# Second pass of the attention scores on 64 rows in each half of TensorE

## The chip, the cores and the metric

The kernel runs on one core of one Trainium2 chip. The metric is the device time of that core in microseconds (us), as the median of several runs. TensorE (PE in the profile) multiplies, VectorE (DVE), ScalarE (ACT) and GpSimd (POOL) do the element work, and SyncE (SP) issues the DMAs.

## The reference

The input `x` has shape (4, 512, 1024). It is layer-normalised to `xn`. An attention block and a gate are computed from `xn`, and the result is `x + attention * silu(gate)`. What the change touches is the scores of the attention, cut here to its core:

```python
q = (xn @ Wq).reshape(b, s, 16, 64)      # likewise k and v; rotary embedding on q and k
logits = einsum('bhqd,bhkd->bhqk', q, k) # 16 heads of dimension 64, 4 batches, 512 tokens
logits = where(causal, logits, -1e9) / sqrt(64)
attn = softmax(logits);  out = einsum('bhqk,bhkd->bhqd', attn, v);  out @ Wo
```

## The kernel before

All products are taken in `float32r`, whose multiplier keeps fewer bits than float32. So an operand is split in a high part (a rounded copy) and a low part (the difference), and a product is the sum high x high + high x low + low x high. `split_matmuls` (L44 to L46) writes these three matmuls for the projections and for the output product.

First the feed-forward block (lines 219 to 286) computes the gate of all tokens and leaves `xn` split in SBUF. Its router product (L231) runs with 32 columns of TensorE for each matmul, four of them beside each other. Then comes the attention loop: 32 steps, one for each pair of heads and each batch (`STEPS`); step `s` projects q, k and v of one pair (`project`, 3 x 8 x 3 matmuls of 128x512), and in between it computes what the projections of step `s-1` made possible: the scores of both heads, the softmax, the transposes of the probabilities (L1110) and their products with v (L1123). Two steps share one set of weights; in the second step of such a couple (`b == 1`) ACT and POOL split the next weights into `w_hi` (L1259) and `w_lo` (L1805). The loop is followed by a tail that finishes the last scores and forms the output product; in step 31 and the tail POOL splits `Wo` (L1809) too.

The scores of one head are causal, so the 128 queries of tile `t` meet `(t+1)*128` keys. `SCORE_BANKS` puts tile 3 (512 wide) in PSUM bank 0, tiles 2 and 0 (384 and 128 wide) in bank 1 and tile 1 (256 wide) in bank 2. The contraction has length 64, but the kernel uses all 128 rows. The stationary `q_st` of head `h` holds the high q on the head's own 64 rows and the low q on the other 64. The moving `k_hh` holds the high k on both halves: one matmul (L1092) gives high x high + low x high. A second one (L1093), with the same `q_st`, has the moving `k_l0`: the low k on the head's own rows and zeros on the others; it adds high x low. The two follow each other for each tile, and each bank is given free (`scored`) when its tiles are done.

The order of each engine is written out by hand in its `step`. What matters around the change:

- PE: projection 0 (first half), `v_transposes` (L1077), two probability transposes, projection 0 (second half), `values`, **`scores(s-1, 0)`**, projection 1, **`scores(s-1, 1)`**, eight transposes, projection 2 and so on. `scores` waits for `qk_ready` (two signals a step) and for the `Exp` of the bank's earlier use.
- DVE: `v_low` (L1516), `pt_low_parts` (L1544, 256 wide), `rotate_read(s, 0)` (L1498, L1499; it waits for projection 0), `merge` (L1552), the maxima of the scores (L1527), `normalise` (L1533, L1537), `q_low` (L1504; first `qk_ready`), `rotate_read(s, 1)`, the second head's maxima, `k_low` (L1511; second `qk_ready`), `pt_low_parts`.
- ACT: `exps` (L1297), `q_high` (L1266), `next_weights` of q in the steps with `b == 1`, the copies of the transposed probabilities (L1306), `k_high` (L1272), the other two `next_weights` (L1259), `v_hi` (L1286).
- POOL: `rotate` (L1797, L1801) of q and k, and in the steps with `b == 1` `weights_low` three times (L1805); the last two of these run into the next step.

The SP queue issues the weights' loads and the stores of each step. In the tail `load_rows(0)` waits for the last `qk_ready` and stands in that queue behind `load_wo(7)` and ahead of `load_att(2)` and the next stores.

Of the kernel before, what the change touches and what calls it, by code (L numbers as in the profile page):

```python
# [6 lines left out]
F32R = mybir.dt.float32r  # L7
ALU = mybir.AluOpType
ACT = mybir.ActivationFunctionType
AX = mybir.AxisListType  # L10

P = 128
# [23 lines left out]
def raw(ap):  # L36

    return ap.bitcast(F32)
# [670 lines left out]
def attention_block(nc, block, io, keep, xn, xn_store, z_store, att_store, out):  # L709
# [5 lines left out]
    with ExitStack() as ctx:  # L715
# [14 lines left out]
        with ExitStack() as loop_only:  # L730
            def lsb(name, shape, dt):
                return loop_only.enter_context(nc.sbuf_tensor(name, shape, dt))

            rotated = [lsb(f"at_rotated{c}", [P, SEQ], F32) for c in range(2)]
            v_t = lsb("at_v_t", [P, SEQ], F32)

            qk = lsb("at_qk", [P, 2, 6, SEQ], F32R)
            q_st, k_hh, k_l0 = ([[qk[:, p, c + h, :] for h in range(2)] for p in range(2)] for c in (0, 2, 4))

            v_hl = [lsb(f"at_v_hl{p}", [P, QT, 4, HEAD_DIM], F32R) for p in range(2)]  # L740
            neg_max = [lsb(f"at_neg_max{h}", [P, QT], F32) for h in range(2)]
            row_sum = [lsb(f"at_row_sum{h}", [P, QT], F32) for h in range(2)]
            inv_sum = [lsb(f"at_inv_sum{h}", [P, QT], F32) for h in range(2)]
            prob = [lsb(f"at_prob{h}", [P, 1280], F32) for h in range(2)]
            pt_hi = [lsb(f"at_pt_hi{h}", [P, 1280], F32R) for h in range(2)]
            pt_lo = [lsb(f"at_pt_lo{h}", [P, 1280], F32R) for h in range(2)]
            low_half = lsb("at_low_half", [P, SEQ], F32)
            att_t = [lsb(f"at_att_t{p}", [P, SEQ], F32) for p in range(2)]
            causal = lsb("at_causal", [P, SEQ], F32)
# [25 lines left out]
        w_high, w_ready, rope_in = keep["w_high"], keep["w_ready"], keep["rope_in"]  # L775

        xn_in, xn_ok = sem("at_xn_in"), keep["xn_ok"]
        zeroed = sem("at_zeroed")
        projected = sem("at_projected")
        rot_read, rot_a, rot_done = sem("at_rot_read"), sem("at_rot_a"), sem("at_rot_done")  # L780
        high_done, qk_ready = sem("at_high_done"), sem("at_qk_ready")
# [272 lines left out]
        def _(pe):  # L1054
# [25 lines left out]
            def scores(a, h, parity):  # L1080
                n = 2 * a + h
                pe.wait_ge(qk_ready, 2 * a + 2)
                if not later(a, 2):
                    pe.wait_ge(zeroed, 4)
                for bank, tiles in enumerate(SCORE_BANKS):
                    if later(n, 1):
                        pe.wait_ge(expd, 3 * (n - 1) + bank + 1)
                    for t, col in tiles:
                        width = (t + 1) * P
                        out = score_ps[bank][:, col:col + width]  # L1090
                        q = q_st[parity][h][:, t * P:(t + 1) * P]
                        pe.matmul(out, q, k_hh[parity][h][:, 0:width], start=True, stop=False)  # L1092
                        last = pe.matmul(out, q, k_l0[parity][h][:, 0:width], start=False, stop=True)  # L1093
                    last.then_inc(scored, 1)

            def prob_transposes(n, h, uses):
# [156 lines left out]
        def _(act):  # L1253
# [7 lines left out]
            def q_high(s, b):  # L1261
                act.wait_ge(rot_done, 2 * s + 1)
                if later(s, 2):
                    act.wait_ge(scored, 6 * (s - 1))
                for h, rows in enumerate(pair_rows):
                    last = act.activation(q_st[b][h][rows, :], rotated[0][rows, :], ACT.Copy)  # L1266
                last.then_inc(high_done, 1)

            def k_high(s, b, h):
                act.wait_ge(rot_done, 2 * s + 2)  # L1270
# [222 lines left out]
        def _(dve):  # L1493
            def rotate_read(s, c):
                dve.wait_ge(projected, 3 * s + c + 1)
                if later(s, 1):
                    dve.wait_ge(rot_done, 2 * s + c - 1)
                dve.tensor_tensor(turned[c][:], proj_ps[c][:], rope[:, 2 * c, :], ALU.mult)  # L1498
                dve.stream_shuffle(swapped[c][:], proj_ps[c][:], swap_mask).then_inc(rot_read, 1)  # L1499
# [8 lines left out]
            def k_low(s, b):  # L1508
                dve.wait_ge(high_done, 2 * s + 2)
                for h, rows in enumerate(pair_rows):  # L1510
                    last = dve.tensor_tensor(k_l0[b][h][rows, :], rotated[1][rows, :], raw(k_hh[b][h][rows, :]), ALU.subtract)  # L1511
                last.then_inc(qk_ready, 1)

            def v_low(a, parity):
# [4 lines left out]
            def maxima(n, h, banks=(0, 1, 2)):  # L1519
                for bank in banks:  # L1520
                    tiles = SCORE_BANKS[bank]
                    dve.wait_ge(scored, 3 * n + bank + 1)
                    dve.sem_inc(seen, 1)
                    dve.wait_ge(causal_ok, 2)
                    for t, col in tiles:
                        row = score_ps[bank][:, col:col + (t + 1) * P]
                        last = dve.tensor_tensor_reduce(out=row, in0=row, in1=causal[:, (QT - 1 - t) * P:SEQ], scale=-1.0,  # L1527
                                                        scalar=FAR, op0=ALU.add, op1=ALU.min, accum_out=neg_max[h][:, t:t + 1])
                    last.then_inc(maxed, 1)
# [10 lines left out]
            def pt_low_parts(n, h, uses=(0, 1, 2)):  # L1540
                for u in uses:
                    dve.wait_ge(pt_high, 3 * n + u + 1)
                    cols = slice(512 * u, 512 * u + PT_WIDTH[u])
                    dve.tensor_tensor(pt_lo[h][:, cols], pt_ps[u % 2][:, 0:PT_WIDTH[u]], raw(pt_hi[h][:, cols]),  # L1544
                                      ALU.subtract).then_inc(pt_ready, 1)
# [8 lines left out]
            def step(i, s, b):  # L1554
                if later(s, 1):
                    v_low(s - 1, 1 - b)
                if later(s, 2):
                    pt_low_parts(2 * s - 3, 1, (2,))
                rotate_read(s, 0)
                if later(s, 2):  # L1560
                    merge(s - 2, 2 * s - 3, 1, b)
                if later(s, 1):
                    maxima(2 * s - 2, 0)
                    normalise(2 * s - 2, 0)
                q_low(s, b)
                rotate_read(s, 1)
                if later(s, 1):
                    maxima(2 * s - 1, 1, (0,))
                    pt_low_parts(2 * s - 2, 0, (0,))
                    maxima(2 * s - 1, 1, (1, 2))  # L1570
                    pt_low_parts(2 * s - 2, 0, (1, 2))
                    normalise(2 * s - 1, 1)
                k_low(s, b)
                if later(s, 1):
                    pt_low_parts(2 * s - 1, 1, (0, 1))
                    merge(s - 1, 2 * s - 2, 0, 1 - b)

            dve.wait_ge(keep["z_add"], BATCH * QT)
            for p in range(2):
                dve.memset(raw(k_l0[p][0][HEAD_DIM:P, :]), 0.0).then_inc(zeroed, 1)  # L1580
                dve.memset(raw(k_l0[p][1][0:HEAD_DIM, :]), 0.0).then_inc(zeroed, 1)
            def wo_lo(k):
                dve.wait_ge(wo_high, k + 1)
                dve.tensor_tensor(wo_part[k][PLO], wo_raw[:, k % 3, :], raw(wo_part[k][PHI]), ALU.subtract).then_inc(wo_low_dve, 1)
# [1 line left out]
            def last_step(s, b):  # L1586

                v_low(s - 1, 1 - b)
                pt_low_parts(2 * s - 3, 1, (2,))
                rotate_read(s, 0)  # L1590
                merge(s - 2, 2 * s - 3, 1, b)
                maxima(2 * s - 2, 0)
                normalise(2 * s - 2, 0)
                q_low(s, b)
                rotate_read(s, 1)
                maxima(2 * s - 1, 1, (0,))
                pt_low_parts(2 * s - 2, 0, (0,))
                maxima(2 * s - 1, 1, (1, 2))
                pt_low_parts(2 * s - 2, 0, (1,))
                wo_lo(3)  # L1600
                pt_low_parts(2 * s - 2, 0, (2,))
                normalise(2 * s - 1, 1)
                k_low(s, b)
                pt_low_parts(2 * s - 1, 1, (0, 1))
# [108 lines left out]
            merge(s - 2, 2 * s - 4, 0, 0)  # L1713
            v_low(s - 1, 1)
            pt_low_parts(2 * s - 3, 1, (2,))
            maxima(2 * s - 2, 0)
            normalise(2 * s - 2, 0)
            merge(s - 2, 2 * s - 3, 1, 0)
# [75 lines left out]
        def _(pool):  # L1794
            def rotate(s, c):
                pool.wait_ge(rot_read, 2 * s + c + 1)
                pool.tensor_tensor(swapped[c][:], swapped[c][:], rope[:, 2 * c + 1, :], ALU.mult).then_inc(rot_a, 1)  # L1797
                pool.wait_ge(rot_a, 2 * s + c + 1)
                if later(s, 1):
                    pool.wait_ge(qk_ready, 2 * s + c - 1)  # L1800
                pool.tensor_tensor(rotated[c][:], swapped[c][:], turned[c][:], ALU.add).then_inc(rot_done, 1)  # L1801

            def weights_low(idx, m):
# [51 lines left out]
def later(count, least):  # L1855

    return not isinstance(count, int) or count >= least
# [94 lines left out]
```

## Time and profile before

| what | us |
|---|---|
| median of 3 runs (1139.3 to 1139.48) | 1139.34 |
| the profiled execution, its own time | 1140.27 |
| its span in the trace | 1138.5 |
| PE busy in the span | 1107.5 |
| DVE busy | 798.3 |
| ACT busy | 639.6 |
| POOL busy | 385.2 |

The rows further below come from the trace of the profiled execution, with times in us from the start of its span. Each row of a timeline is one instruction, or several of one kind merged (`x2`); its first number is its start and its second the time from there to the end. The duration that is shown for a matmul is modelled and overlaps the next one: what a matmul costs is read from one start to the next. `PEld` are the weight loads of TensorE; `[1.40 <-PE at_proj L46]` is idle time of the engine before the row and what ended it.

### The profile page before, as it was taken

What the parts mean: (1) busy time and instruction counts of PE and PEld (TensorE: products, weight loads), DVE (VectorE), ACT (ScalarE), POOL (GpSimd) and SP (SyncE); (2) the same over time, 40 slices, a digit from 0 to 9 for tenths busy, and PEclk for the clock granted to TensorE, in tenths of its full rate; (3) what the DMA queues carried; (4) which work ended last, traced back from release to release, by engine and by line L of the source; (5) the groups of instructions that cost most, each with busy time, mean ns of one, the idle gap of its engine ahead of it and who ended that gap; (6) DMA issues with size and microseconds to landing.
All of it is one profiled execution on the core that took longest, in us unless ns stands there. A gap on an engine that the chain in (4) does not pass through costs nothing.

```text
span 1138.5 us, 17762 instructions
## 1 busy us (share of the span) xinstructions
PE 1107.5 (97%) x5620; PEld 925.2 (81%) x5620; DVE 798.3 (70%) x1860; ACT 639.6 (56%) x1344; POOL 385.2 (34%) x240
## 2 busy tenths in 40 slices
PE   4899999999999999999999999999999999999998
PEld 3667777888888888888888888888888887788887
DVE  6768641476767776767776677767677768899865
ACT  6545542366665666646566565666656667645341
POOL 0443646352342433334342352523424335200000
PEclk9899999999999999999999999999999999999999
DMA  9526133220202202021460202202022014586764
GB/s 368 209 93 241 55 94 111 75 65 11 64 9 74 64 10 64 9 64 49 172 221 9 64 18 64 64 9 64 9 74 64 10 64 168 188 282 219 235 212 148
DMA packets 88719, 116.40 MB, mean 102 GB/s; under 512 B 3440, under 2 KB 69104, under 8 KB 87664
## 3 DMA queue, kind: packets, MB, share of 16 engines
q1 hardware_dynamic: 88688, 116.01, 30.4%
q8 instruction: 16, 0.26, 0.1%
q14 instruction: 15, 0.12, 0.0%
HBM read 82.44 MB, written 33.55 MB: 102 GB/s over the span
## 4 chain that ended last, share of the span: by engine, by line
PE 87%; DVE 6%; ACT 3%; issue 1%; POOL 1%; DMA 1%; SPq 0%; DVEq 0%; POOLq 0%; ACTq 0%
PE at_proj L44 17%; PE at_proj L46 17%; PE at_proj L45 17%; PE at_out L1123 7%; PE at_pt L1110 6%; PE ff_z_ps L286 5%; PE at_score L1092 4%; PE at_score L1093 3%; POOL ff_xs_lo L669 1%; PE at_pt L44 1%; PE at_pt L46 1%; PE at_pt L45 1%; PE at_proj L1077 1%; PE at_score L44 1%; PE at_score L45 1%
## 5 line engine op out<-in xcount | busy, mean ns | idle before, releaser
L44 PE MATMUL at_proj<-xn_hi,w_hi 128*128 128x512 f32 x824 | 333.6, 405 | 1.6 <-POOL w_lo L1813 0.8
L46 PE MATMUL at_proj<-xn_hi,w_lo 128*128 128x512 f32 x824 | 322.8, 392 | 0.0
L45 PE MATMUL at_proj<-xn_lo,w_hi 128*128 128x512 f32 x824 | 321.3, 390 | 0.0
L46 PEld LDWEIGHTS at_proj<-xn_hi,w_lo 128*128 128x128 f32 x824 | 154.6, 188 | 34.5
L1797 POOL TENSOR_TENSOR at_turning<-at_turning,rope_table 128x512 f32<-128x512 f32 x64 | 82.8, 1294 | 289.4 <-DVE at_turning L1499 289.4
L44 PEld LDWEIGHTS at_proj<-xn_hi,w_hi 128*128 128x128 f32 x824 | 154.9, 188 | 29.1 <-issue 1.2
L45 PEld LDWEIGHTS at_proj<-xn_lo,w_hi 128*128 128x128 f32 x824 | 155.3, 188 | 27.5
L1297 ACT ACTIVATE at_prob<-at_score,at_neg_max 128x512 f32<-128x512 f32 (+3 forms) x256 | 133.5, 526 | 71.2 <-DVE at_neg_max L1527 70.8
L1805 POOL TENSOR_TENSOR w_lo<-w_stage,w_hi 128x1024 fp32r<-128x1024 f32 x45 | 114.4, 2558 | 162.9 <-ACT w_hi L1259 162.9
L1306 ACT ACTIVATE at_pt_hi<-at_pt 128x512 fp32r<-128x512 f32 (+1 forms) x192 | 94.0, 524 | 99.7 <-PE at_pt L1110 98.9
L1544 DVE TENSOR_TENSOR at_pt_lo<-at_pt,at_pt_hi 128x512 fp32r<-128x512 f32 (+1 forms) x192 | 112.1, 598 | 42.1 <-ACT at_pt_hi L1306 41.1
L1527 DVE CUSTOM_DVE_ANT_0 at_score<-at_score,at_causal 128x512 f32<-128x512 f32 (+3 forms) x256 | 120.8, 514 | 1.0
L1110 PE MATMUL at_pt<-ident,at_prob 128*128 128x128 f32 x640 | 91.7, 274 | 0.8 <-DVE at_pt_lo L1544 0.6
L1313 ACT ACTIVATE at_low_half<-at_out 64x512 f32<-64x512 f32 x64 | 37.9, 592 | 96.8 <-PE at_out L1123 96.0
L1801 POOL TENSOR_TENSOR at_rotated<-at_turning 128x512 f32<-128x512 f32 x64 | 82.8, 1293 | 7.3 <-POOL at_turning L1797 4.4
L1511 DVE TENSOR_TENSOR at_qk<-at_rotated,at_qk 64x512 fp32r<-64x512 f32 x64 | 45.1, 705 | 56.4 <-ACT at_qk L1272 56.0
L286 PE MATMUL ff_z_ps<-sign_t,ff_xs_hi 128*128 128x512 f32 x256 | 83.4, 407 | 0.8 <-POOL ff_xs_lo L669 0.8
L1537 DVE TENSOR_SCALAR at_prob<-at_prob,at_inv_sum 128x256 f32<-128x256 f32 (+3 forms) x256 | 82.0, 384 | 2.3
L1272 ACT ACTIVATE at_qk<-at_rotated 64x512 fp32r<-64x512 f32 x128 | 80.5, 629 | 1.8 <-POOL at_rotated L1801 0.2
L286 PE MATMUL ff_z_ps<-sign_t,ff_xs_lo 128*128 128x512 f32 x256 | 81.4, 399 | 0.0
L1092 PE MATMUL at_score<-at_qk 128*128 128x512 f32 (+3 forms) x256 | 80.5, 328 | 0.0
L1110 PEld LDWEIGHTS at_pt<-ident,at_prob 128*128 128x128 f32 x640 | 73.0, 141 | 6.6 <-DVE at_pt_lo L1544 1.6
(214 smaller groups left out, 1924.9 us busy)
## 6 DMA issues: line engine op xcount, KB each, us to landing
w_stage<-_attn_hidden_states_dram SPq DMA_DIRECT2D x17, 512.0 KB, 6.4
z_store<-z SPq DMA_DIRECT2D x16, 512.0 KB, 2.8
w_stage<-in_L_attn_Wq_dram SPq DMA_DIRECT2D x16, 512.0 KB, 3.8
w_stage<-in_L_attn_Wk_dram SPq DMA_DIRECT2D x16, 512.0 KB, 5.1
w_stage<-in_L_attn_Wv_dram SPq DMA_DIRECT2D x16, 512.0 KB, 6.2
att_store<-at_att_t SPq DMA_DIRECT2D x32, 256.0 KB, 2.0
at_turning<-z_store SPq DMA_DIRECT2D x16, 512.0 KB, 5.4
w_stage<-in_L_attn_Wo_dram SPq DMA_DIRECT2D x12, 512.0 KB, 4.3
```

The costliest lines, as they stand in the source:

```text
L44: pe.matmul(out, sh, mh, start=first, stop=False, skip_group_check=reopened)
L45: pe.matmul(out, sh, ml, start=False, stop=False, skip_group_check=reopened)
L46: return pe.matmul(out, sl, mh, start=False, stop=final, skip_group_check=reopened)
L286: last = pe.matmul(z_ps[n % 2][:, o, :], part[:, k, tok], keep["sign_t"][:, k, o * HALF:(o + 1) * HALF], start=(k == 0 and part is xs_hi), ...
L1092: pe.matmul(out, q, k_hh[parity][h][:, 0:width], start=True, stop=False)
L1110: last = pe.transpose(pt_ps[u % 2][:, dst:dst + P], prob[h][:, src:src + P], keep["ident"][:])
L1297: last = act.activation(prob[h][:, P_COL[t]:P_COL[t] + width], score_ps[bank][:, col:col + width], ACT.Exp, scale=-1.0, bias=neg_max[h][:, ...
L1306: act.activation(pt_hi[h][:, 512 * u:512 * u + PT_WIDTH[u]], pt_ps[u % 2][:, 0:PT_WIDTH[u]], ACT.Copy).then_inc(pt_high, 1)
L1527: last = dve.tensor_tensor_reduce(out=row, in0=row, in1=causal[:, (QT - 1 - t) * P:SEQ], scale=-1.0, scalar=FAR, op0=ALU.add, op1=ALU.min, ...
L1544: dve.tensor_tensor(pt_lo[h][:, cols], pt_ps[u % 2][:, 0:PT_WIDTH[u]], raw(pt_hi[h][:, cols]), ALU.subtract).then_inc(pt_ready, 1)
L1797: pool.tensor_tensor(swapped[c][:], swapped[c][:], rope[:, 2 * c + 1, :], ALU.mult).then_inc(rot_a, 1)
L1805: pool.tensor_tensor(w_lo[m][:], w_raw[m], raw(w_hi[m][:]), ALU.subtract).then_inc(w_ready[m], 1)
```

## The change

The high part of q and both parts of k stay as they are in `q_st` and `k_hh`. The zero-padded `k_l0` is gone, with the four memsets that wrote its zeros. In its place are `k_own` (the low k of both heads, each on its own rows), `k_other` (the low k of each head, the first 384 keys, on the rows of the other head) and `q_other` (the high q of tiles 0 and 2 of each head, on the rows of the other head). The first pass of `scores` now makes the four matmuls of L1092 for all tiles, with 128 rows. The second pass makes four matmuls with 64 rows: tiles 3 and 1 on the head's own rows, tiles 2 and 0 on the other rows. `scored` is given in the second pass.

ACT makes two more copies in each `q_high` (64x256 each, behind the two that are there). DVE makes two more subtractions for each step (64x384 each), in the new `k_spread`. The second `qk_ready` of a step is given there; it is called one step later, ahead of `rotate_read(s, 0)`, and in the tail ahead of the maxima. `rotate` on POOL waits for the full `qk_ready` of the step before in both of its calls.

```diff
-            q_st, k_hh, k_l0 = ([[qk[:, p, c + h, :] for h in range(2)] for p in range(2)] for c in (0, 2, 4))
+            q_st, k_hh = ([[qk[:, p, c + h, :] for h in range(2)] for p in range(2)] for c in (0, 2))
+            k_own, k_other = ([qk[:, p, c, :] for p in range(2)] for c in (4, 5))
+            q_other = lsb("at_q_other", [P, 2, 2 * P], F32R)
+            OTHER_COL = {0: 0, 2: P}
+            OTHER_KEYS = 3 * P
...
             def scores(a, h, parity):
                 pe.wait_ge(qk_ready, 2 * a + 2)
...
-                        out = score_ps[bank][:, col:col + width]
-                        q = q_st[parity][h][:, t * P:(t + 1) * P]
-                        pe.matmul(out, q, k_hh[parity][h][:, 0:width], start=True, stop=False)
-                        last = pe.matmul(out, q, k_l0[parity][h][:, 0:width], start=False, stop=True)
+                        pe.matmul(score_ps[bank][:, col:col + width], q_st[parity][h][:, t * P:(t + 1) * P],
+                                  k_hh[parity][h][:, 0:width], start=(col == 0), stop=False, skip_group_check=True)
+                for bank, tiles in enumerate(SCORE_BANKS):
+                    for t, col in tiles:
+                        width = (t + 1) * P
+                        if t in OTHER_COL:
+                            q = q_other[other, parity, OTHER_COL[t]:OTHER_COL[t] + P]
+                            k = k_other[parity][other, 0:width]
+                        else:
+                            q = q_st[parity][h][own, t * P:(t + 1) * P]
+                            k = k_own[parity][own, 0:width]
+                        last = pe.matmul(score_ps[bank][:, col:col + width], q, k, start=False, stop=True,
+                                         skip_group_check=True)
                     last.then_inc(scored, 1)
...
             def q_high(s, b):
...
+                for h, rows in enumerate(pair_rows):
+                    act.activation(q_other[pair_rows[1 - h], b, :].rearrange("p (t n) -> p t n", t=2),
+                                   rotated[0][rows, :].rearrange("p (t a n) -> p t a n", t=2, a=2)[:, :, 0, :], ACT.Copy)
...
             def k_low(s, b):
                 dve.wait_ge(high_done, 2 * s + 2)
                 for h, rows in enumerate(pair_rows):
-                    last = dve.tensor_tensor(k_l0[b][h][rows, :], rotated[1][rows, :], raw(k_hh[b][h][rows, :]), ALU.subtract)
+                    dve.tensor_tensor(k_own[b][rows, :], rotated[1][rows, :], raw(k_hh[b][h][rows, :]), ALU.subtract)
+
+            def k_spread(b):
+                for h, rows in enumerate(pair_rows):
+                    last = dve.tensor_tensor(k_other[b][pair_rows[1 - h], 0:OTHER_KEYS], rotated[1][rows, 0:OTHER_KEYS],
+                                             raw(k_hh[b][h][rows, 0:OTHER_KEYS]), ALU.subtract)
                 last.then_inc(qk_ready, 1)
...
                     pt_low_parts(2 * s - 3, 1, (2,))
+                if later(s, 1):
+                    k_spread(1 - b)
                 rotate_read(s, 0)
...
                 if later(s, 1):
-                    pool.wait_ge(qk_ready, 2 * s + c - 1)
+                    pool.wait_ge(qk_ready, 2 * s)
```

## Rows read from the trace of the kernel before

**Rows 1.** The page, part 1: busy time of TensorE, share, instructions

```profile
PE 1107.5 (97%) x5620; PEld 925.2 (81%) x5620; DVE 798.3 (70%) x1860; ACT 639.6 (56%) x1344; POOL 385.2 (34%) x240
```

**Rows 2.** Windows, five steps: stretch, length, busy PE PEld DVE ACT POOL, clock, DMA

```profile
400.00:520.00 120.00, 120.00 (x637) 103.07 (x636) 85.18 (x223) 72.16 (x166) 42.26 (x26) 1.00 0.13 37
```

**Rows 3.** Timeline of PE, the scores of one second head (h = 1)

```profile
613.78 0.39 PE L1092 MATMUL at_score<-at_qk 128*128 128x512 f32 x1
...
614.23 0.33 PE L1092 MATMUL at_score<-at_qk 128*128 128x384 f32 x1
...
614.58 0.22 PE L1092 MATMUL at_score<-at_qk 128*128 128x128 f32 x1
614.64 0.27 PE L1093 MATMUL at_score<-at_qk 128*128 128x128 f32 x1
614.75 0.33 PE L1092 MATMUL at_score<-at_qk 128*128 128x256 f32 x1
614.92 0.28 PE L1093 MATMUL at_score<-at_qk 128*128 128x256 f32 x1
615.04 1.03 PE L1110 MATMUL at_pt<-ident,at_prob 128*128 128x128 f32 x8
```

**Rows 4.** Timelines of PE and PEld, narrow windows: into and out of the 32-column mode

```profile
147.59 0.40 PE L286 MATMUL ff_z_ps<-sign_t,ff_xs_lo 128*128 128x512 f32 x1
147.91 0.64 PE L231 MATMUL ff_small<-xn_full,ff_gate_raw 128*32 128x512 f32 x4
...
149.22 0.61 PE L231 MATMUL ff_small<-xn_full,ff_gate_raw 128*32 128x512 f32 x4
149.77 0.50 PE L286 MATMUL ff_z_ps<-sign_t,ff_xs_hi 128*128 128x512 f32 x1
150.10 0.40 PE L286 MATMUL ff_z_ps<-sign_t,ff_xs_hi 128*128 128x512 f32 x1
...
149.76 0.19 PEld L286 LDWEIGHTS ff_z_ps<-sign_t,ff_xs_hi 128*128 128x128 f32 x1 [0.84 <-issue]
```

**Rows 5.** Timeline of DVE: two steps of the loop, step 31, tail

```profile
606.05 0.69 DVE L1498 TENSOR_TENSOR at_turning<-at_proj,rope_table 128x512 f32<-128x512 f32 x1 [1.40 <-PE at_proj L46]
...
623.80 1.39 DVE L1511 TENSOR_TENSOR at_qk<-at_rotated,at_qk 64x512 fp32r<-64x512 f32 x2 [1.65 <-ACT at_qk L1272]
...
628.66 0.42 DVE L1544 TENSOR_TENSOR at_pt_lo<-at_pt,at_pt_hi 128x256 fp32r<-128x256 f32 x1
...
942.94 0.41 DVE L1544 TENSOR_TENSOR at_pt_lo<-at_pt,at_pt_hi 128x256 fp32r<-128x256 f32 x1
...
952.25 3.47 DVE L1504 TENSOR_TENSOR at_qk<-at_rotated,at_qk 64x512 fp32r<-64x512 f32 x2
...
969.05 0.42 DVE L1544 TENSOR_TENSOR at_pt_lo<-at_pt,at_pt_hi 128x256 fp32r<-128x256 f32 x1
```

**Rows 6.** Timeline of POOL: the splits of the weights (w_lo) and of Wo

```profile
626.66 4.75 POOL L1805 TENSOR_TENSOR w_lo<-w_stage,w_hi 128x1024 fp32r<-128x1024 f32 x2 [7.22 <-ACT w_hi L1259]
...
943.74 2.42 POOL L1809 TENSOR_TENSOR xn_lo<-w_stage,xn_hi 128x1024 fp32r<-128x1024 f32 x1 [10.51 <-ACT xn_hi L1318]
...
952.29 2.88 POOL L1809 TENSOR_TENSOR xn_lo<-w_stage,xn_hi 128x1024 fp32r<-128x1024 f32 x1 [1.15 <-DVE at_prob L1537]
...
967.42 2.40 POOL L1809 TENSOR_TENSOR xn_lo<-w_stage,xn_hi 128x1024 fp32r<-128x1024 f32 x1 [2.13 <-ACT xn_hi L1318]
```

**Rows 7.** Timeline of PE: first scores of a first head, three steps

```profile
631.18 0.45 PE L1092 MATMUL at_score<-at_qk 128*128 128x512 f32 x1
...
945.69 0.45 PE L1092 MATMUL at_score<-at_qk 128*128 128x512 f32 x1
...
968.35 0.48 PE L1092 MATMUL at_score<-at_qk 128*128 128x512 f32 x1
```

**Rows 8.** ACT: q_high's copies by line, and its next idle time

```profile
L1266 ACT ACTIVATE at_qk<-at_rotated x64: 623/628/632, 207.2 to 950.9; 64x512 fp32r<-64x512 f32 x64
...
615.68 1.09 ACT L1306 ACTIVATE at_pt_hi<-at_pt 128x512 fp32r<-128x512 f32 x2 [1.80 <-PE at_pt L1110]
```

More of the change, by code:

```diff
@@ L777, in attention_block @@
         xn_in, xn_ok = sem("at_xn_in"), keep["xn_ok"]
-        zeroed = sem("at_zeroed")
         projected = sem("at_projected")
@@ L1082, in scores @@
                 pe.wait_ge(qk_ready, 2 * a + 2)
-                if not later(a, 2):
-                    pe.wait_ge(zeroed, 4)
+                own, other = pair_rows[h], pair_rows[1 - h]
                 for bank, tiles in enumerate(SCORE_BANKS):
@@ L1578, in _ @@
             dve.wait_ge(keep["z_add"], BATCH * QT)
-            for p in range(2):
-                dve.memset(raw(k_l0[p][0][HEAD_DIM:P, :]), 0.0).then_inc(zeroed, 1)
-                dve.memset(raw(k_l0[p][1][0:HEAD_DIM, :]), 0.0).then_inc(zeroed, 1)
             def wo_lo(k):
@@ L1589, in last_step @@
                 pt_low_parts(2 * s - 3, 1, (2,))
+                k_spread(1 - b)
                 rotate_read(s, 0)
@@ L1715, in _ @@
             pt_low_parts(2 * s - 3, 1, (2,))
+            k_spread(1)
             maxima(2 * s - 2, 0)
```

## The prediction

> **What bounds the kernel now.** I read the page's shares first, then the windows of the loop, then the timeline of one step on each engine, and last the timelines where the loop ends. TensorE is busy for 97% of the span, DVE for 70%, ACT for 56% [rows 1]; in five steps of the loop TensorE has no idle time at all, at the full clock (granted 1.00, which is 2.4 GHz), while DVE is busy for 85.18 of 120 us, ACT for 72.16 and POOL for 42.26 [rows 2]. So in the loop the order of TensorE sets the time: whatever a step takes more or less there counts in full, and work of the other engines costs nothing as long as no wait of TensorE ends later for it. The change does something on both sides, so I price TensorE's instructions first and then look for the new waits.
>
> **The second pass on 64 rows.** A head's scores run from 613.78 to 615.04, 1.26 us [rows 3]. From starts: two 512-wide matmuls 0.45 (0.23 and 0.22), two 384-wide 0.35, the first 128-wide 0.06, the second 0.11, 256-wide 0.17 and 0.12. The weight loads explain the odd ones: a matmul that follows a 128-wide one comes only after about 0.11, since its load takes longer than 128 columns. After the change the first pass is 512, 384, 128, 256 in a row: 0.23 + 0.17 + 0.11 + 0.12 = 0.63. The second pass, if the halves work beside each other, is the longer of 0.23 (512, own rows) and 0.17 + 0.06 (384 and 128, other rows), then 256 on the own rows at 0.12: 0.35. Together 0.98, which is 0.28 less than now. Times 64 heads that is 17.9 us, the most that the halves can give.
>
> The trace has no 64-row matmul. The nearest thing is the router product, which runs in a mode of 128 rows and 32 columns [rows 4]. It shows that parts do work beside each other: four 512-wide matmuls start together at 147.91. It also shows what entering and leaving costs. Going in: the last full matmul starts at 147.59 and streams for 0.23, to 147.82; the first of the mode starts at 147.91, 0.09 later. Going out: the last four start at 149.22; between groups of four there are 0.43 us, so they end at 149.65; the next full-size weight load starts at 149.76 and not in the shade of the matmuls before it, 0.11 of nothing; the second full matmul follows the first by 0.33 instead of 0.23, so the load itself is exposed, 0.10 to 0.11. Each direction then costs 0.09 to 0.11 of emptiness and a full load of 0.11 that nothing hides. For one head: in 0.09 + 0.11, out 0.11 + 0.11, together 0.42. The head's scores become 0.63 + 0.20 + 0.35 + 0.22 = 1.40, against 1.26: **0.14 more for each head, 64 x 0.14 = 9.0 us**. Bounds: nothing for the mode gives -17.9; halves that do not overlap make the second pass 0.64 instead of 0.35, 0.43 a head more than now, +27.5. I take +9.0, as the only change of mode in the trace is priced like that.
>
> On this the Trainium skill, TensorEngine Tiling (Array Packing), Key Properties, says that changing the tiling mode drains TensorE while changing the tile does not. By that rule the switch costs in rows as in columns, and the trace agrees for columns, with the 0.09 and 0.11 us above; no row here shows it for rows.
>
> **k_spread on DVE.** Two subtractions of 64x384, both operands in SBUF. A pair of 64x512 takes 1.39, at 623.80 [rows 5], so one is about 0.69; 128x256 takes 0.42; 384 wide lies between, 0.56, and the pair is 1.13. Its place is behind `pt_low_parts` and ahead of `rotate_read(s, 0)`. In an odd step DVE idles there for 1.40, ahead of 606.05 [rows 5], so the pair fits: nothing. In an even step the idle time would nearly do as well, but POOL is at work: it splits the last two weights from 626.66 to 631.41 [rows 6], and k_spread is ready at 629.0, which is 628.66 + 0.42 less the overlap of two instructions [rows 5].
>
> What happens to a DVE instruction with two SBUF operands while POOL runs such a split is shown where the loop ends. The pair of q_low that starts at 952.25 takes 3.47 instead of 1.39; POOL's split started at 952.29 and ended at 955.17, and the pair ends at 955.72, 0.55 behind it [rows 5, 6]. The first of the pair got through, POOL took 2.88 instead of 2.40, and the second waited for POOL's end. So the later of the two waits for the earlier one. In even steps of the loop no DVE instruction with both operands in SBUF meets POOL's last two splits today; k_spread will. Either both of its parts wait for 631.41 and end at 631.41 + 0.42 + 0.57 = 632.40, or the first slips in between the two splits and the second waits for the delayed one, 631.9 + 0.42 = 632.3. `scores(s-1, 0)` waits for that signal, and TensorE is ready for it at 631.18 [rows 7]. With about 0.05 for the signal and 0.06 for a load that can't be hidden, TensorE stands for 632.40 + 0.11 - 631.18 = 1.3 us. POOL's pair of splits is 4.75 long and ends 0.23 to 0.25 behind that start of the scores in all 15 even steps from s = 2 to s = 30: **15 x 1.3 = 19.5 us**. Queued behind k_spread on DVE are `rotate_read`, `merge` and the maxima; they come some 2 us late, TensorE itself 1.4 late, and DVE's idle times later in the step (1.65 ahead of L1511 [rows 5]) take up the difference. Bounds: 0, if DVE and POOL don't hold each other up (k_spread ends at 630.2, before 631.18), and 1.4 for each even step.
>
> The Trainium skill, SBUF — State Buffer, Summary: rules for kernel authors, has the same rule: with two SBUF inputs on DVE while GpSimd reads SBUF, the second to issue is fully blocked until the first is done. The trace agrees (3.47 instead of 1.39 us).
>
> **Where the loop ends.** In step 31 POOL splits Wo from 943.74 to 946.16 [rows 6] and k_spread comes at 943.3 [rows 5]: its second part waits and ends at about 946.65, against scores that start at 945.69 [rows 7]: 1.1 us. In the tail nothing stands between k_spread and the scores: DVE comes to it at 969.4, which is 969.05 + 0.42 less the overlap [rows 5], POOL splits until 969.82 [rows 6], k_spread ends at 969.82 + 0.42 + 0.57 = 970.8, and the scores that started at 968.35 [rows 7] start at 970.85: 2.5 us. DVE's chain behind them (maxima, normalise) is the one that TensorE next waits for, another 0.4. Sum **4.0 us**; bounds 1.5 (k_spread alone behind 969.4, with no wait for POOL) and 5.
>
> **The rest, at nothing.** The two extra ACT copies of 64x256: a 64x512 one takes 0.63 [rows 8], so they are 0.42 each at most, 0.84 for both. They come behind q_high, where ACT later idles 1.80 for TensorE [rows 8]; POOL's first split in odd steps starts 0.8 later and is out of q_low's way. If that cover were gone, the transposes' copies would come up to 0.84 late, at worst once a step. `scored` for bank 0 comes 0.63 + 0.20 + 0.23 = 1.06 behind the first matmul instead of 0.45, for bank 2 at 1.18 instead of 1.26; DVE is busy with merge or rotate_read until then. The four memsets and the wait for them are gone, ahead of the loop: nothing. No DMA is added. `load_rows(0)` on SP's queue waits for the last k_spread, half a microsecond beyond its present issue, and its rows are wanted much later. POOL's stricter wait holds nothing, since its first operation waits for `rotate_read`, which is behind k_spread anyway.
>
> **Sum.** 1140.27 (the profiled execution) + 9.0 + 19.5 + 4.0 = 1172.8; the median of the runs is 0.9 lower, so 1171.9. I say 1172.
>
> **Rivals.** A, the other side: the copies get through beside POOL and changing between row modes costs little, so the halves give all they can: 1139.3 - 17.9 = 1121. It turns at k_spread's end: before 631.1, nothing waits; the profile speaks for the room (1.2 to 1.4 us of idle time for 1.13), and against it are the 3.47 us pair and the exposed loads of rows 4. Chance 0.11. B: the copies are held up as I say, but TensorE changes between 128 and 64 rows for nothing: 1139.3 - 17.9 + 23.5 = 1145. For it: no row shows a change of rows only. 0.18. C: nothing held up on DVE, but the modes cost their 0.14 a head: 1139.3 + 9.0 = 1148. 0.06. D: the halves do not overlap, all else as forecast: 1139.3 + 27.5 + 23.5 = 1190. That the change doesn't do what it says; against it are the four matmuls that start together. 0.09. My forecast, with its own range from 1160 to 1182 (partial hiding of the loads one way, a load between the 384- and the 128-wide tile on the other rows that nothing hides, 0.1 a head, the other way): 0.56.
>
> **How the numbers follow.** Leaving out A at the bottom and D at the top, 0.20 together, the range is 1143 to 1184. A measurement of this kernel tells about 0.2% (2.3 us) from no change. Faster has A and a point of the mixtures between A and B: 0.12; the same 0.02; slower 0.86.
>
> **What would show it.** The modes: the stretch of a second head from its first score matmul to the first transpose, 1.40 (0.98 if they are free, 1.69 if the halves don't overlap), and weight loads of the 64-row matmuls that do not start ahead of the end of the first pass. The copies: k_spread's pair in even steps over 3 us long and in odd steps 1.1, and TensorE idle before the first score matmul of each even step, about 1.2 us, released by DVE; in the tail 2.5. I am wrong if PE's idle time in the loop stays at nothing, or if the h = 1 stretch is shorter than 1.26.

## The result and the profile after

The changed kernel takes 1172.28 us as median of 4 runs (1171.55 to 1176.0), against 1139.32 us before; the ratio is 1.0297, with a 95% interval from 1.0275 to 1.0319. That is 33 us more. The profiled execution took 1172.76 us, with a span of 1171.0 us. The forecast was 1172. One execution of one experiment, the one on the head's own rows, took 1586.72 us at a mean granted clock of 0.655; the medians and ratios below leave it out.

The first part of the page of the changed kernel answers to [rows 1]:

```profile
PE 1121.6 (96%) x5620; PEld 914.2 (78%) x5620; DVE 867.8 (74%) x1920; ACT 664.7 (57%) x1408; POOL 378.0 (32%) x240
```

Its windows of five steps, with the columns of [rows 2], show where it happened: TensorE is busy for 117.60 of 120 us and no longer for all of them, with the same clock, and DVE does more.

```profile
400.00:520.00 120.00, 117.60 (x617) 97.77 (x616) 92.20 (x223) 73.06 (x168) 37.50 (x24) 1.00 0.16 46
```

Its list of waits (who waited for whom, us in total, times, longest) has one that was not there before:

```profile
PE at_score L1093 <- DVE at_qk L1530: 21.0, 17, 2.2
```

TensorE's score matmuls (L1093) waited for k_spread (L1530) 17 times: in the 15 even steps from 2 to 30, in step 31 and in the tail. One of these waits in full, in an even step of the changed kernel, answers to [rows 5 to 7]. The timeline of PE:

```profile
645.56 0.27 PE L1135 MATMUL at_out<-at_pt_lo,at_v_hl 128*128 128x128 f32 x1
647.03 0.90 PE L1093 MATMUL at_score<-at_qk 128*128 128x512 f32 x4 [1.20 <-DVE at_qk L1530]
```

The timeline of DVE, first in that step and then in an odd one:

```profile
643.13 0.41 DVE L1564 TENSOR_TENSOR at_pt_lo<-at_pt,at_pt_hi 128x256 fp32r<-128x256 f32 x1
643.58 3.30 DVE L1530 TENSOR_TENSOR at_qk<-at_rotated,at_qk 64x384 fp32r<-64x384 f32 x2
...
619.01 1.12 DVE L1530 TENSOR_TENSOR at_qk<-at_rotated,at_qk 64x384 fp32r<-64x384 f32 x2
```

The timeline of POOL:

```profile
641.14 4.76 POOL L1826 TENSOR_TENSOR w_lo<-w_stage,w_hi 128x1024 fp32r<-128x1024 f32 x2 [6.99 <-ACT w_hi L1271]
```

POOL splits until 645.90; k_spread is issued at 643.58, waits, and its pair ends at 646.88, 0.98 behind POOL; 0.15 later the scores start. In the odd step, where POOL is idle, the same pair takes 1.12. The `pt_low_parts` just ahead of k_spread is a subtraction on DVE too, but one of its operands is in PSUM; it took 0.41 while POOL was splitting, as it does elsewhere (0.42 at 942.94 of the kernel before, with POOL idle).

The idle time that the row names, 1.20, is less than what is lost: it is counted from the modelled end of the matmul before. From starts, the last product with v is at 645.56, and the scores would follow 0.11 behind it, as they do before; they come 1.47 behind, 1.36 later. Their first load lies bare too, another 0.05 (the second score matmul follows the first by 0.34, and by 0.29 where there is no wait). So one wait is 1.41 us.

The second pass, in the scores of a second head of the changed kernel, answers to [rows 3]. The timeline of PE:

```profile
628.24 0.39 PE L1093 MATMUL at_score<-at_qk 128*128 128x512 f32 x1
...
628.96 0.49 PE L1104 MATMUL at_score<-at_qk 64*128 64x512 f32 x1
628.96 0.44 PE L1104 MATMUL at_score<-at_qk,at_q_other 64*128 64x384 f32 x1
629.24 0.22 PE L1104 MATMUL at_score<-at_qk,at_q_other 64*128 64x128 f32 x1
629.29 0.27 PE L1104 MATMUL at_score<-at_qk 64*128 64x256 f32 x1
629.49 0.33 PE L1122 MATMUL at_pt<-ident,at_prob 128*128 128x128 f32 x1
...
630.34 0.48 PE L44 MATMUL at_proj<-xn_hi,w_hi 128*128 128x512 f32 x1
```

The timeline of the weight loads in the same stretch:

```profile
628.95 0.18 PEld L1104 LDWEIGHTS at_score<-at_qk 64*128 64x128 f32 x1
628.96 0.18 PEld L1104 LDWEIGHTS at_score<-at_qk,at_q_other 64*128 64x128 f32 x1
...
629.49 0.14 PEld L1122 LDWEIGHTS at_pt<-ident,at_prob 128*128 128x128 f32 x1 [0.24 <-issue]
```

The 512- and the 384-wide matmul start together, and so do their loads: the halves do work beside each other. But no load starts ahead of the change of mode, neither at 628.95 nor at 629.49. From the first score matmul to the projection behind the transposes it is 2.10 us, against 2.05 before (613.78 to 615.83). For a first head it is worse, since full-size work follows at once: from the first score to the second projection matmul 1.67 instead of 1.55. The timeline of PE in the changed kernel:

```profile
621.32 0.45 PE L1093 MATMUL at_score<-at_qk 128*128 128x512 f32 x1
...
622.99 0.40 PE L45 MATMUL at_proj<-xn_lo,w_hi 128*128 128x512 f32 x1
```

and in the kernel before:

```profile
606.99 0.45 PE L1092 MATMUL at_score<-at_qk 128*128 128x512 f32 x1
...
608.54 0.39 PE L45 MATMUL at_proj<-xn_lo,w_hi 128*128 128x512 f32 x1
```

### The profile page after: what moved, and what is told of

Read it like the earlier page. It is cut to its first block, busy times and chain, and to the rows that moved or that the text cites. A ratio compares the mean times of both kernels' runs of the same rounds, so it can differ in the third digit from the quotient of the medians.

```text
span 1171.0 us, 17885 instructions
## 1 busy us (share of the span) xinstructions
PE 1121.6 (96%) x5620; PEld 914.2 (78%) x5620; DVE 867.8 (74%) x1920; ACT 664.7 (57%) x1408; POOL 378.0 (32%) x240
## 4 chain that ended last, share of the span: by engine, by line
PE 73%; DVE 9%; ACT 9%; issue 6%; POOL 2%; DMA 1%; ACTq 0%; SPq 0%; DVEq 0%
PE at_proj L44 15%; PE at_proj L46 14%; PE at_proj L45 14%; PE ff_z_ps L286 5%; PE at_pt L1122 5%; PE at_score L1093 4%; PE at_out L1135 3%; PE at_score L1104 3%; DVE at_qk L1530 3%; ACT w_hi L1271 2%; ACT at_qk L1287 2%; POOL ff_xs_lo L669 1%; PE at_pt L45 1%; PE at_pt L44 1%; PE at_pt L46 1%
## 5 line engine op out<-in xcount | busy, mean ns | idle before, releaser
L44 PE MATMUL at_proj<-xn_hi,w_hi 128*128 128x512 f32 x824 | 337.7, 410 | 1.6 <-POOL w_lo L1834 0.8
L1826 POOL TENSOR_TENSOR w_lo<-w_stage,w_hi 128x1024 fp32r<-128x1024 f32 x45 | 107.4, 2400 | 173.8 <-ACT w_hi L1271 173.8
L1135 PE MATMUL at_out<-at_pt_hi,at_v_hl 128*128 128x512 f32 (+3 forms) x256 | 76.9, 312 | 1.4 <-issue 0.8
```

What stands on the lines that cost most here:

```text
L44: pe.matmul(out, sh, mh, start=first, stop=False, skip_group_check=reopened)
L1135: last = pe.matmul(out_ps[:, kt * P:SEQ], v, part[h][:, cols], start=(kt == 0 and part is pt_hi), stop=(kt == QT - 1 and part is pt_lo))
L1826: pool.tensor_tensor(w_lo[m][:], w_raw[m], raw(w_hi[m][:]), ALU.subtract).then_inc(w_ready[m], 1)
```

## The experiments

**The copies alone.** The kernel before, with the change's copies written into tiles that nothing reads, and with POOL's stricter wait in `rotate`.

```diff
                 for h, rows in enumerate(pair_rows):
-                    last = dve.tensor_tensor(k_l0[b][h][rows, :], ...)
-                last.then_inc(qk_ready, 1)
+                    dve.tensor_tensor(k_l0[b][h][rows, :], ...)
+            def k_spread(b):        # as in the change, into a tile of its own; called one step later
+                ...
+                last.then_inc(qk_ready, 1)
```

> The kernel before, with its two full-row matmuls for each tile, plus the change's copies alone: ACT's two 64x256 copies and DVE's k_spread one step later write tiles that no matmul reads, and the second qk_ready waits for k_spread. My theory (DVE's two-operand copies meet POOL's weight split and are held up by it, TensorE waits for them 17 times, 21 us in the trace after): 1139.3 + 21 = 1160 to 1162 us, with TensorE idle 1.2 us before the first scores of each even step. Rival U (the copies lie in idle time of DVE and ACT; the change of modes makes all 33 us, some 0.5 us a head): 1139 to 1142 us.

Measured: 1164.94 us, ratio 1.0226 (1.0209 to 1.0243). The waits are the same 17 with 21.1 us in the list. The two weight splits of POOL recur after 49.80 us instead of 48.39, 1.41 more for each couple of steps; 15 of them make 21.2. The rest of the 25.8 us, 4.6, lies in step 31 and the tail. Rival U is out. The expectation was 3 us low, because I took the listed idle time for the loss: 15 waits of 1.41 and not 1.2 are 3 us more.

**The halves alone.** The changed kernel with `q_other` and `k_other` zeroed once and no copies; it leaves out the high x low term of tiles 2 and 0.

```diff
-                if later(s, 1):
-                    k_spread(1 - b)
...
+            for p in range(2):
+                dve.memset(raw(k_other[p]), 0.0).then_inc(zeroed, 1)
+            dve.memset(raw(q_other[:]), 0.0).then_inc(zeroed, 1)
```

> The changed kernel without its copies: the second pass runs on 64 rows in the two halves as in the change, but q_other and k_other are zeroed once ahead of the loop and never written again (so the high x low term of tiles 2 and 0 is left out), and qk_ready comes from k_low as before. My theory: no wait on DVE is left, and each head pays about 0.13 to 0.18 us for going into the 64-row mode and out of it: 1139.3 + 64 x 0.13..0.18 = 1148 to 1151 us. Rival U (modes cost 0.5 a head): 1170 us. Rival V (modes are free and the halves give 0.28 a head): 1121 us.

Measured: 1144.96 us, ratio 1.0049 (1.0032 to 1.0066): 5.8 us more than before, 0.09 us a head. By the period of a couple it is 48.71 against 48.39, 0.32 for four heads, 0.08 each. Modes that are free (V) and modes at 0.5 a head (U) are both out. The measured time lies under my own range of 1148 to 1151: my figure for a head was too high.

**All four on the head's own rows.** The changed kernel without its copies, and with the full result.

```diff
-                        if t in OTHER_COL:
-                            q = q_other[...]; k = k_other[...]
-                        else:
-                            q = q_st[parity][h][own, ...]; k = k_own[parity][own, 0:width]
+                        q = q_st[parity][h][own, t * P:(t + 1) * P]
+                        k = k_own[parity][own, 0:width]
```

> The second pass on 64 rows for all four tiles, but all on the head's own rows, one behind the other: no copies, no second half, the full result. My theory: the same two changes of mode as in halves_only, and 512 columns more in a row for each head, 64 x 0.23 = 15 us: 1163 to 1167 us. Rival W (the two halves do not work beside each other in the changed kernel): the same time as halves_only within 2 us.

Measured: 1162.65 us, ratio 1.0208 (1.0188 to 1.0229), just under my range. It is 17.7 us above the halves, 0.28 a head. So the second half of the array does hide the 384- and the 128-wide tile, and rival W is out.

**The order alone.** Both passes on 128 rows, as before, but the four matmuls with `k_hh` first.

```diff
-                        pe.matmul(out, q, k_hh[parity][h][:, 0:width], start=True, stop=False)
-                        last = pe.matmul(out, q, k_l0[parity][h][:, 0:width], start=False, stop=True)
+                        pe.matmul(..., k_hh[parity][h][:, 0:width], start=(col == 0), stop=False, ...)
+                for bank, tiles in enumerate(SCORE_BANKS):     # a second loop over the banks
+                        last = pe.matmul(..., k_l0[parity][h][:, 0:width], start=False, stop=True, ...)
```

> The kernel before with only the order of the passes changed: the four matmuls with k_hh first, then the four with k_l0, all on 128 rows. My theory: the order alone costs nothing, 1138.5 to 1140.5 us. Rival X (a bank's scores coming later holds up DVE's maxima and so the chain behind them): over 1141 us.

Measured: 1138.92 us, ratio 1.0 (0.999 to 1.0009). The order costs nothing. In the loop it even saves a little (48.33 us for a couple of steps instead of 48.39), and the tail gives 0.5 us of that back.

**ACT's copies alone.** The kernel before with the two 64x256 copies behind q_high, into an unread tile.

```diff
+                for h, rows in enumerate(pair_rows):
+                    act.activation(q_other[pair_rows[1 - h], b, :]..., rotated[0][rows, :]..., ACT.Copy)
```

> The kernel before plus only the change's two 64x256 copies on ACT, into a tile that nothing reads. My theory: hidden in ACT's idle time, 1138.5 to 1140 us. Rival: they push POOL's first split and the copies behind them, and carry the 2 to 4 us by which copies_only is over the sum of its waits: 1141 to 1143 us.

Measured: 1139.39 us, ratio 1.0001 (0.9992 to 1.0011). They are hidden.

**POOL steps aside.** The changed kernel with one wait added, none taken away.

```diff
                     weights_low(i + 1, 1)
+                    pool.wait_ge(qk_ready, 2 * s + 2)
                     weights_low(i + 1, 2)
```

> The changed kernel with one wait more, on POOL: in the loop its third weight split waits until k_spread of the step before is done, so that k_spread meets only the second split, which ends about when k_spread is ready. Nothing is taken away from DVE, ACT or TensorE. My theory (DVE and POOL hold each other up): k_spread's pair takes 1.1 to 1.2 us in the even steps too, the 15 waits of TensorE in the loop (1.42 us each against the kernel before, by the starts of the traces) go, those of step 31 and of the tail stay: 1172 - 21 to 23 = 1149 to 1152 us. Rival Y (k_spread is late for its own length or for where it stands in DVE's order): no gain, 1170 us or more.

Measured: 1150.29 us, ratio 1.0096 (1.0079 to 1.0113). It is inside my range. This is the clearest run on the cause: nothing was taken from DVE, and POOL was made later, yet 22 us are gone. The timelines in an even step of this kernel show why; k_spread takes 1.12 between two splits, and the third split starts behind it. DVE:

```profile
679.39 1.12 DVE L1530 TENSOR_TENSOR at_qk<-at_rotated,at_qk 64x384 fp32r<-64x384 f32 x2
```

POOL:

```profile
676.96 2.40 POOL L1826 TENSOR_TENSOR w_lo<-w_stage,w_hi 128x1024 fp32r<-128x1024 f32 x1 [7.00 <-ACT w_hi L1271]
680.67 2.39 POOL L1826 TENSOR_TENSOR w_lo<-w_stage,w_hi 128x1024 fp32r<-128x1024 f32 x1 [1.31 <-DVE at_qk L1530]
```

Its list of waits has two left on k_spread, in step 31 and in the tail:

```profile
PE at_score L1093 <- DVE at_qk L1530: 3.1, 2, 2.2
```

**k_spread straight behind k_low.**

```diff
-                if later(s, 1):
-                    k_spread(1 - b)
                 rotate_read(s, 0)
...
                 k_low(s, b)
+                k_spread(b)
```

> The changed kernel with k_spread straight behind k_low in the same step, instead of a step later. POOL is idle there in both kinds of step. My theory: no wait of TensorE on k_spread is left, in the tail neither; what stays is the price of the modes (5.8 us in halves_only) and up to 1 us where DVE's parts behind it come 1.1 us later: 1144 to 1147 us. Rival Z (the place a step earlier pushes pt_low_parts so far that TensorE waits for them, 0.3 us or more a step): over 1154 us.

Measured: 1150.58 us, ratio 1.0097 (1.008 to 1.0114), over my range and under the rival's. TensorE no longer waits for k_spread, but a couple of steps takes 49.05 us and not 48.71. `pt_low_parts` comes 1.1 us later, and the transposes that wait for it start 0.53 behind those of v instead of 0.43; the next projection 0.20 behind instead of 0.14. PE in this kernel:

```profile
655.47 0.60 PE L1081 MATMUL at_proj<-ident,at_v_t 128*128 128x128 f32 x4
656.00 0.44 PE L1122 MATMUL at_pt<-ident,at_prob 128*128 128x128 f32 x2
656.20 0.48 PE L44 MATMUL at_proj<-xn_hi,w_hi 128*128 128x512 f32 x1
```

and in the changed kernel:

```profile
388.96 0.60 PE L1081 MATMUL at_proj<-ident,at_v_t 128*128 128x128 f32 x4
389.39 0.38 PE L1122 MATMUL at_pt<-ident,at_prob 128*128 128x128 f32 x2
389.53 0.47 PE L44 MATMUL at_proj<-xn_hi,w_hi 128*128 128x512 f32 x1
```

That is 0.16 us a step, too short for the list of waits, since matmuls' modelled ends hide it, and 5 us in 32 steps. So the step of delay in the change does buy something; it pays for it where POOL is at work.

**k_other filled by ACT.** DVE has no part in it; ACT copies `k_own` to the other rows.

```diff
+            def k_spread(a, b):      # on ACT, behind the copy of the last transposes
+                act.wait_ge(qk_ready, 2 * a + 2)
+                for h, rows in enumerate(pair_rows):
+                    last = act.activation(k_other[b][pair_rows[1 - h], 0:OTHER_KEYS], raw(k_own[b][rows, 0:OTHER_KEYS]), ACT.Copy)
+                last.then_inc(k_copied, 1)
```

> The changed kernel with k_other filled by ACT as a copy of k_own (two 64x384 copies, 0.5 us each, behind the copy of the last transposes of the step before), so that DVE has no part in it. My theory: ACT has no quarrel with POOL, so no wait is left in the loop: 1144 to 1148 us, with up to 1 us of waits in step 31 and the tail. Rival Y' (any copy in this place of the step is too late for the scores): 1155 us or more.

Measured: 1146.06 us, ratio 1.0058 (1.0041 to 1.0074). A couple takes 48.71, as with the halves alone, and here with the full result. No wait for the copies is listed any more. The 1.1 us over the halves alone are one wait in step 31, for the low part of the probabilities, which is not there with the halves alone:

```profile
963.30 0.44 PE L1124 MATMUL at_pt<-ident,at_prob 128*128 128x128 f32 x2 [1.02 <-DVE at_pt_lo L1572]
```

The kernel still is 6.7 us over the one before. No version with the halves beat the kernel before, and the experiments do not point to one: what is left is the price of the modes.

## Why the prediction was right, step by step

The sum was 9.0 + 19.5 + 4.0 = 32.5 us, and 33.0 was measured. The mechanism was as forecast; that the sum came within 0.5 us is luck, since its terms were off by more than that, in both directions.

- **The wait for k_spread in the loop** was forecast at 15 x 1.3 = 19.5 and is 21.2, 15 times 1.41 (copies alone). Its mechanism is as forecast: the pair ends 0.98 behind POOL (0.99 forecast), takes 1.12 where POOL is idle (1.13 forecast), and goes with POOL's split moved. The signal and the start of TensorE take 0.15 where I had 0.05; the rest of the working is right to 0.01.
- **Step 31 and the tail** were forecast at 4.0 and cost 4.6 in the copies alone. In step 31 the wait was 1.1 by starts, as forecast. In the tail it was 2.2 (2.5 forecast), and hardly for POOL: k_spread took 1.24 there in the changed kernel and 1.28 in the copies alone, and the wait is its place in DVE's order. The chain of DVE was put at 0.4; it shows in step 31, where the next transposes wait 0.98 for the low part of the probabilities in the copies alone, and 0.12 before.
- **The modes** were forecast at 0.14 a head, 9.0 in all. They cost 0.09 a head, 5.8. The term of the sum that was mis-sized is the way out, 0.22 a head: 0.11 of drain and a full bare load of 0.11. The drain is some 0.09. Behind a second head come 128-wide transposes, whose loads were half bare before the change as well (8 of them took 0.79; now 0.85), so the load costs 0.06 there. Only behind a first head is the whole load a new cost. The rest of the working held: first score to first matmul of the mode 0.72 (0.63 + 0.09 forecast), and the second pass with its first load and the drain behind it 0.53 (0.11 + 0.35 + 0.11 forecast), in which the 128-wide tile's load was hidden.
- **The sign for the modes** was set wrongly. The prediction wanted 1.40 us from the first score of a second head to its first transpose, and called itself wrong under 1.26. Measured are 1.25 (628.24 to 629.49), against 1.26 before, and the modes cost time all the same. The 1.40 have in them the bare load of the way out, which lies behind the recorded start of the first transpose; from start to start the working gives 1.29. In the stretch itself the two drains and the first load just use up the 0.28 that the halves save, and what is lost lies behind it.
- **The rest at nothing**: right for the order (1138.92) and for ACT's copies (1139.39).
- **What made up for the modes** is two things. The loop's waits were 1.7 over the forecast, and TensorE's clock, which the sum did not have, fell twice (last section). By the starts of the scores, the 32.5 us between the two spans are, but for rounding: 27.2 up to the scores in step 30 (21.3 with the copies alone, 4.6 with the halves alone); 4.6 from there to the first scores of the tail (4.5 and 0.2); 1.7 behind them (-0.1 and 0.8); and -1.1 ahead of the first scores (218.91 against 219.97). What the two experiments don't have between them, 1.3 us in the loop and 1.0 behind the tail's first scores, lies where the clock fell.

Rival A fell with the copies alone, B and C with the same pair of runs, of which each has one of the two costs and both are real; D fell with the own rows.

That DVE and POOL hold each other up made 21 of the 33 us: the pair of k_spread took 3.30 us beside the split and 1.12 without it. The Trainium skill, SBUF — State Buffer, Summary: rules for kernel authors, says that a DVE instruction with two SBUF inputs and a GpSimd one that reads SBUF exclude each other, the second to issue being blocked until the first is done; the trace agrees.

A change between 128 and 64 rows empties TensorE as the change of columns did: the first load of the mode starts at 628.95, when the 256-wide matmul before it, at 628.70, had been through for some 0.1 us (an estimate from the rows: its load from 628.64, then 0.11 for it and 0.11 for the columns, 628.86). The Trainium skill, TensorEngine Tiling (Array Packing), Key Properties, says that a change of the tiling mode drains TensorE; the trace now agrees for rows too.

## What to carry to other kernels

A gap on an engine is cover only for work that may run there: before a copy goes into it, look at what the other engines do in that stretch, and whether one of them holds the copy up, in every kind of step of the loop, since here the same gap was free in odd steps and closed in even ones. Work on half the rows pays when what it saves is more than a drain and a bare weight load each way; hiding 512 columns a head was not enough. Longer runs of matmuls in the mode might be, which no run here shows. A change of mode also costs behind the stretch that runs in it, so measure up to the second matmul of the work that follows. When TensorE has no slack, take a wait's price from starts, not from the idle time in a list.

## What the runs showed of the hardware that was not expected

A short wait of TensorE can be followed by a fall of its clock. In the changed kernel the wait ahead of 394.95 (1.20 idle, the same as in the other even steps) is followed, 2.0 us after it ends, by a lower granted clock, though TensorE is busy in between. In the windows of the changed kernel the last column but two falls to 0.50, which is 1.2 instead of 2.4 GHz:

```profile
396.00:397.00 1.00, 1.00 (x7) 0.66 (x6) 0.94 (x3) 0.00 (x0) 0.74 (x1) 0.96 0.00 0
397.00:398.00 1.00, 1.00 (x4) 0.81 (x3) 0.98 (x3) 0.14 (x1) 0.92 (x2) 0.50 0.04 14
```

In its timeline of PE matmuls of 512 columns then follow each other by 0.42 us instead of 0.23:

```profile
397.28 0.63 PE L44 MATMUL at_proj<-xn_hi,w_hi 128*128 128x512 f32 x1
397.70 0.63 PE L45 MATMUL at_proj<-xn_lo,w_hi 128*128 128x512 f32 x1
```

That couple of steps took 51.69 us instead of 50.10. In the tail it came again behind the wait of 2.19 (0.50 from 1002 to 1004), and in the trace of POOL stepping aside behind the wait of 2.22 in the same place. In the copies alone, a wait of 2.23 us in that place left the clock at 1.00, and so did its other 16. So of the 36 waits on k_spread in the three traces 3 were followed by a fall. Between the first scores and the end of the tail no other fall stands in the ten traces, though waits of 0.8 us for other things stand in all of them. That the wait brings the fall is likely by this and not shown.

It goes with the spread of this kernel: its four runs have mean clocks of 0.991, 0.993, 0.995 and 0.995 and times of 1176.0, 1172.8, 1171.8 and 1171.6. What decides whether the clock falls stays open.
